# Attention and mixture-of-experts block on 8 cores: a second context buffer, and one output-projection block in each of four head pairs instead of four in the first

## The reference, cut to what matters

```python
def reference(x, w_qkv, w_out, w1, b1, w2, b2, wr, br):
    xn = _layernorm(x)
    # attention: 16 heads of 64, causal, S = 2048
    q, k, v = split(xn @ w_qkv.T)
    scores = einsum('bhqd,bhkd->bhqk', q, k) / 8
    attn = softmax(where(causal, scores, -1e30))
    out = einsum('bhqk,bhkd->bhqd', attn, v)
    a = concat_heads(out) @ w_out.T
    # feed-forward: 4 experts of hidden size 4096, top 2 by router logits
    gates, idx = softmax(top_k(xn @ wr + br, 2))
    y = gelu(xn @ w1[e] + b1[e]) @ w2[e] + b2[e]     # for each expert e
    c = gelu(b1) @ w2 + b2
    f = sum_k gates_k * (y[idx_k] - c[idx_k] + c.sum(0))
    return x + a + f
```

## Time and profile before

| | us |
|---|---|
| two runs | 3293.16 and 3294.1, median 3293.63 |
| profiled execution | 3289.5 |
| span of its slowest core (core 3) | 3288.0 |
| spans of the 8 cores | 3276.5 to 3288.0 |

### The profile page before, as it was taken

One profiled execution on the slowest core, in us unless ns is written; L12 is line 12 of the kernel. 1 busy time (PEld: TensorE's weight loads), 2 busy tenths in 40 slices (PEclk: granted clock), 3 DMA queues, 4 the chain that ended last, 5 costly groups with the idle time before them and its releaser, 6 DMA issues. The chain is left out here.

```text
span 3288.0 us, 30066 instructions; the slowest of 8 cores (3276.5 to 3288.0 us)
## 1 busy us (share of the span) xinstructions
PE 2828.4 (86%) x11124; PEld 1082.2 (33%) x11124; DVE 784.8 (24%) x1052; ACT 861.4 (26%) x1164; POOL 35.6 (1%) x60
## 2 busy tenths in 40 slices
PE   2479867778878886999999999999999999999970
PEld 0134311111111112444444444444444444444420
DVE  4441453322221111111111111121111121111224
ACT  1122154545545552111222221112222211112100
POOL 0000000000000000000000000000000000000000
PEclk9689856565575557999999999999999999999955
DMA  8610100000000105033033113303321330230016
GB/s 150 104 29 1 26 0 26 0 26 0 0 26 0 26 0 102 1 52 52 1 52 52 23 30 52 52 1 52 52 32 21 52 52 6 46 52 1 1 45 262
DMA packets 79677, 127.86 MB, mean 39 GB/s; under 512 B 36142, under 2 KB 36270, under 8 KB 79282
## 3 DMA queue, kind: packets, MB, share of 16 engines
q0 software_dynamic: 33600, 75.50, 15.0%
q1 hardware_dynamic: 45938, 50.44, 4.9%
HBM read 176.26 MB, written 25.17 MB: 61 GB/s over the span
## 5 line engine op out<-in xcount | busy, mean ns | idle before, releaser
L828 PE MATMUL P<-xn_fm,w1g 128*128 128x512 bf16 x4096 | 897.3, 380 | 24.3 <-PEq L43 24.3
L859 PE MATMUL P<-w2g,h_sb 128*128 128x512 bf16 x4096 | 894.3, 379 | 0.0
L836 ACT ACTIVATE h_sb<-P,b_sb 128x512 bf16<-128x512 f32 x512 | 351.9, 687 | 1445.7 <-PE P L828 1445.7
L878 DVE SCALAR_TENSOR_TENSOR accum<-P,agate,accum 128x1024 f32<-128x1024 f32 x240 | 308.1, 1284 | 1379.8 <-PE P L859 1379.8
L828 PEld LDWEIGHTS P<-xn_fm,w1g 128*128 128x128 bf16 x4096 | 400.1, 98 | 513.0 <-issue 35.0
L859 PEld LDWEIGHTS P<-w2g,h_sb 128*128 128x128 bf16 x4096 | 400.8, 98 | 483.3
L676 ACT ACTIVATE p_sb<-P,cneg 128x1024 bf16<-128x1024 f32 x320 | 353.2, 1114 | 405.0 <-PE P L668 404.6
L697 PE MATMUL P<-p_sb,v_ext 128*65 128x512 bf16 x320 | 191.4, 598 | 123.8 <-DVE p_sb L684 65.5
L704 PE MATMUL P<-p_sb,v_ext 128*65 128x512 bf16 x320 | 194.4, 608 | 0.0
L684 DVE TENSOR_TENSOR p_sb<-p_sb,masks 128x1024 bf16<-128x1024 bf16 x128 | 87.9, 690 | 407.3 <-ACT p_sb L676 407.3
L668 PE MATMUL P<-q_fm,k_fm 64*128 64x512 bf16 x320 | 175.7, 608 | 0.0
(11 more groups left out here) (108 smaller groups left out, 940.6 us busy)
## 6 DMA issues: line engine op xcount, KB each, us to landing
w1g<-w POOLq DMA_DIRECT2D x16, 2048.0 KB, 17.5
w2g<-w POOLq DMA_DIRECT2D x16, 2048.0 KB, 27.9
xA<-x SPq DMA_DIRECT2D x4, 2048.0 KB, 27.0
attn_sc<-proj SPq DMA_DIRECT2D x16, 512.0 KB, 2.6
xrg<-x SPq DMA_DIRECT2D x4, 2048.0 KB, 9.7
arg<-attn_sc SPq DMA_DIRECT2D x4, 2048.0 KB, 14.2
y<-outr SPq DMA_DIRECT2D x16, 512.0 KB, 2.9
wqkv_bf<-w_qkv POOLq DMA_DIRECT2D x3, 2048.0 KB, 45.4
```

The costliest lines, as they stand in the source:

```text
L828: t.matmul(PH67[par][:, 0:512], w1g[buf][:, dc * 1024 + hc * 128:dc * 1024 + (hc + 1) * 128], xn_fm[:, dc * 2048 + tt * 512:dc * 2048 + (t ...
L836: s.activation(h_sb[tt % 2][:, hc * 512:(hc + 1) * 512], PH67[par][:, 0:512], AF.Gelu, bias=b1_sb[:, e_ * 32 + g_ * 8 + hc:e_ * 32 + g_ * ...
L859: pt=pt, st=st, sp=sp: t.matmul(pt[:, half * 512:(half + 1) * 512], h_sb[tt % 2][:, hc * 512 + ts4 * 128:hc * 512 + (ts4 + 1) * 128], w2g[ ...
L878: v.scalar_tensor_tensor(accum[:, tsg * 1024:(tsg + 1) * 1024], pt[:, 0:1024], agate[:, tsg * 4 + e_:tsg * 4 + e_ + 1], accum[:, tsg * 102 ...
```

## The change

A second context buffer `attn_cat2` is added, and the tiles alternate between the two (0 and 2 write `attn_cat`, 1 and 3 write `attn_cat2`). L647 now waits for the last block of the tile two before. To make room in SBUF, `w_outT` moves down by 2048 bytes, and three small buffers move with it. The rule that places the blocks changes: one block behind step 0 of each pair until the list is empty, so in tiles 1 to 3 the four blocks stand in pairs 0, 1, 2 and 3. A loop at the last pair would empty the list, but it is empty by then. The four blocks of tile 3 stay at the end.

```diff
-    w_outT = at("w_outT", [128, 8192], BF16, 188928)
+    w_outT = at("w_outT", [128, 8192], BF16, 186880)
...
+    attn_cat2 = at("attn_cat2", [128, 4096], BF16, 203264)
...
-        if qt_ > 0:
-            W("vector", "ST", v_outproj[qt_ - 1])
-        v_am = I("vector", "SV", lambda v, head=head, pair=pair, hr=hr, sl=sl:
-                 v.tensor_tensor(
-                     attn_cat[hr:hr + 64, pair * 512:(pair + 1) * 512],
+        if qt_ >= 2:
+            W("vector", "ST", v_outproj[qt_ - 2])
+        ac = attn_cat if qt_ % 2 == 0 else attn_cat2
+        v_am = I("vector", "SV", lambda v, head=head, pair=pair, hr=hr, sl=sl,
+                 ac=ac: v.tensor_tensor(
+                     ac[hr:hr + 64, pair * 512:(pair + 1) * 512],
                      sl[0:64, :], rbsb[head % 2][:], ALU.mult))
...
+        ac = attn_cat if qt_src % 2 == 0 else attn_cat2
...
-                               attn_cat[:, ec * 512 + ts4 * 128:ec * 512 + (ts4 + 1) * 128],
+                               ac[:, ec * 512 + ts4 * 128:ec * 512 + (ts4 + 1) * 128],
...
-                if op_defer and i_hp == 0:
+                if op_defer and p == 0:
                     op_defer.pop(0)()
             if pending[0] is not None:
                 flush_stage2(pending[1])
-            while op_defer and i_hp == 0:
+            while op_defer and i_hp == NH // 2 - 1:
                 op_defer.pop(0)()
```

More of the change, by code:

```diff
@@ L150, in build_nc @@
     rbr0 = at("rbr0", [1, 512], BF16, 180736)
-    rbr1 = at("rbr1", [1, 512], BF16, 182784)
-    rbsb0 = at("rbsb0", [64, 512], F32, 184832)
-    rbsb1 = at("rbsb1", [64, 512], F32, 186880)
+    rbr1 = at("rbr1", [1, 512], BF16, 181760)
+    rbsb0 = at("rbsb0", [64, 512], F32, 182784)
+    rbsb1 = at("rbsb1", [64, 512], F32, 184832)
     proj0 = at("proj0", [128, 1024], F32, 172544)
@@ L728, in emit_opuser @@
                     E("tensor", lambda t, ts4=ts4, ec=ec, half=half, st=st,
-                      sp=sp, pb=pb:
+                      sp=sp, pb=pb, ac=ac:
                       t.matmul(pb[:, half * 512:(half + 1) * 512],
-                               attn_cat[:, ec * 512 + ts4 * 128:ec * 512 + (ts4 + 1) * 128],
+                               ac[:, ec * 512 + ts4 * 128:ec * 512 + (ts4 + 1) * 128],
                                w_outT[:, ec * 1024 + half * 512:ec * 1024 + (half + 1) * 512],
                                start=st, stop=sp))
-        v_op = I("tensor", "ST", lambda t, ts4=ts4, pb=pb:
+        v_op = I("tensor", "ST", lambda t, ts4=ts4, pb=pb, ac=ac:
                  t.matmul(pb[:, 512:1024],
-                          attn_cat[:, 7 * 512 + ts4 * 128:7 * 512 + (ts4 + 1) * 128],
+                          ac[:, 7 * 512 + ts4 * 128:7 * 512 + (ts4 + 1) * 128],
                           w_outT[:, 7 * 1024 + 512:8 * 1024],
```

## The result

The changed kernel takes 0.9893 of the time of before (95% interval 0.9863 to 0.9923), about 35 us less on the 3293.63 us of before; the interval reaches from 25 to 45 us. Its profiled execution took 3258.51 us, 31.0 less than that of before, with a span of 3257.0 us on its slowest core, core 5. The forecast was 3272 us, 21 less; it had the sign and the mechanism, and its gain was a third too small.

What follows compares the result with a forecast made beforehand. PE at a slow granted clock was taken to bound attention; the tiles' -34 us plus allowances of 5 and 8 gave -21, so 3268.5 profiled and 3272 as median; forecast range 3250 to 3283, chance 0.62.

Steps and rivals of the forecast that it cites:

- The second buffer costs nothing and saves nothing: Second context buffer and moved addresses in attention: removes no wait the trace shows, only makes the new places legal; 0 us.
- A lone block's own time: One block behind step 0 of a pair: 5.0 us if even (first, third), 5.7 if odd (second, fourth).
- The tail at full clock: Steps behind a block to the pair's end run fast: 16.0 us in tile 3's first pair, 16.3 in later ones.
- The pairs of tile 3: Pairs with blocks: first -15.4 us, even -2.6, two odd -1.7 each; tile 3 together -21.4.
- Of tile 2: Pairs with blocks: first -15.0 us, even +0.3, two odd +1.1 each; tile 2 together -12.5.
- Of tile 1: Pairs with blocks: first -10.8 us, even +2.9, two odd +3.7 each; tile 1 together -0.5.
- The allowances: Added to the sum: 5 us for slow tails in tile 1, 8 for clock falls in masked steps of tiles 2 and 3.
- rival A: Clock falls a few us behind each single block in attention, so tails are slow: +25 us, 3319; chance 0.12.
- Rival B: Tails fast only in tile 3's unmasked steps, or in half the pairs: -5 us, 3289; chance 0.20.
- Rival C: Clock outlives the pair's end, so blocks 2 to 4 take 3.45 us: -17 more, -51 in all, 3243; chance 0.06.

Runs made afterwards that it cites:

- The fill: Changed kernel plus matmuls whose result nobody reads in waits of tiles 1 to 3: 0.9538 of before; with the four blocks back in each first pair, 0.9513.

## Why the prediction was right, point by point

- *The second buffer costs nothing and saves nothing*: right, 1.0023 with it alone.
- *A lone block's own time*: 5.0 us for even ones was about right (4.8 from 1004.32 to 1009.11), 5.7 for odd ones was short (6.2). The wait ahead of an odd block was 1.41 us, taken as 1.35, and the 2.5 us behind it came out as 2.54.
- *The tail at full clock*: 16.3 us forecast from the step behind the block to the next pair; measured 979.50 to 995.79, 16.3 us. The plain steps at 2.54 and the masked at 3.33 us carried over unchanged.
- *The pairs of tile 3*: forecast 30.95, 34.9, 34.0, 34.9; measured 31.85, 35.53, 33.24, 35.07. The third is short because the clock was still up for its first 4.4 us, so that its block came after 8.5 us and not 9.0. *Of tile 2*: forecast 25.9, 29.8, 29.0, 29.8; measured 29.18, 31.04, 28.98, 29.28 on the slowest core. *Of tile 1*: 20.9, 24.7, 23.9, 24.7; measured 21.73, 25.33, 25.13, 25.21.
- *The allowances*: these terms were mis-sized, 13 us where the slowest core needed 7.0. Of the 8 us for a clock that falls in the masked steps of tiles 2 and 3 it needed 3.9: in tile 3 no pair lost the clock before its last step, and the tile gave 20.5 us of the 21.4 that stood ahead of the allowance; tile 2 gave 9.5 of 12.5. In tile 2 the clock fell early once, in the first pair, and only on some cores. The stretch behind the rise in tile 2's first block on core 5, in two windows, and on core 7:

```profile
696.40:703.20 6.80, 5.36 (x24) 1.93 (x22) 1.23 (x1) 1.60 (x3) 0.00 (x0) 1.00 0.19 77
703.20:717.87 14.67, 13.25 (x28) 2.09 (x26) 3.45 (x5) 7.35 (x7) 0.00 (x0) 0.50 0.00 0
```

```profile
697.40:717.90 20.50, 12.89 (x51) 3.34 (x49) 5.36 (x7) 12.14 (x12) 0.00 (x0) 1.00 0.06 26
```

  On core 5 the clock fell 6.8 us after its rise, as rival A has it, and the pair took 29.2 us; on core 7 it held, and the pair took 26.3. Tile 2 took 239.7 us on cores 1, 3 and 5, and 235.7 on the other five; why a core goes the one way or the other is open. Of the 5 us for tile 1 the slowest core needed 3.1 (it lost 2.6 us where -0.5 stood ahead of the allowance), and the five others none (183.7 us against 184.6). So the 27.4 us gained in the three tiles stand against 21 forecast. The remaining 3.6 us of the span lie outside, where the forecast had nothing and said that more than 2 us would upset the sum; with cores of one execution 12 us apart there (2577.2 and 2589.8), that limit was too tight.
- *Rival A* (a lone block buys nothing, 3319 us) fell for blocks at a pair's head, but for the first pair of tile 2 on three cores. At the pair's end it was so: +22.6 us in the three tiles, where A had +25. The Trainium skill (TensorE: Matmul & The Clock Gate, section "HAM oscillation — how this bites in real kernels") describes bursts of matmuls between waits for DMA, each of which starts at the slow clock. With the blocks at the pair's end the trace agrees so far, that each of tile 3's four meets the clock at 0.50, though behind the second, which was read, no wait is longer than 1.63 us and none is for DMA. In the changed kernel each of the twelve blocks of the slowest core meets it at 0.50 too, and those of tile 3 paid for themselves by the work right behind them.
- *Rival B* (a draw) fell: 0.9893 with an interval that ends at 0.9923.
- *Rival C* (the clock outlives the pair's end) fell as forecast for the change: on the slowest core it was lost 4.5 us into the next pair at the latest, so never as late as the next block. The fill made it true for most pairs, and then it was worth far more than its 17 us more, since it also makes all the pairs without a block fast.

## What to carry to other kernels

Read the granted clock by stage before counting instructions: here the same pair of heads takes 36.6 us at clock 0.50 and 26.7 at 1.00, with more matmuls in it. Where waits between matmuls cost TensorE its clock, dense work belongs at the head of the longest stretch of plain steps and not at its end (0.9893 against 1.0107 here); better still, fill the waits at the place where the clock is lost, with real work if there is any and with matmuls that nobody reads if not (only the latter was tried here). Count them, though: the fill with more matmuls brought nothing clear beyond this one. Try such fill without reordering anything first: it made this kernel 4.9% faster, against 1.1% for the careful placing of real blocks.

## What was not expected

- The waits that lose the clock are short. PE at the start of the third pair of tile 3 in the changed kernel, where the clock fell at 1000.20:

```profile
997.91 0.38 PE L699 MATMUL P<-p_sb,v_ext 128*65 128x512 bf16 x1 [1.51 <-ACT p_sb L678]
...
1000.10 0.51 PE L637 MATMUL P<-rbr,ones_bf 1*64 1x512 bf16 x1 [1.60 <-ACT rbr L631]
...
1002.39 0.61 PE L699 MATMUL P<-p_sb,v_ext 128*65 128x512 bf16 x1 [0.81 <-DVE attn_cat L649]
```

  None of them is over 1.60 us, and 11 matmuls in these three places kept the clock at 0.96 and 0.91 in the two pairs shown above, and at 0.79 or more in every pair of tile 3 on every core.
- The same program ran with the clock rising and falling at different places, core by core: 26.3 or 29.2 us for the same pair in one execution. A forecast of a single pair from one core's rows could not be closer than that here.
- Work can have a negative price: 16 useless matmuls made a pair 3.4 to 3.8 us shorter (36.6 to 33.2, 36.1 to 32.3, 36.6 to 32.8).
